# Slot scores transposed in one float32r product, and a running sum scanned along tokens, in a hybrid attention layer on one Trainium2 core

## The reference, cut to what matters

```python
s = hs @ Ws1.T @ Ws2.T + bs2                      # rank 16, then 16 heads x 64 slots
s = clip(s, -32, 32)                              # per head: [tokens, 64]
z = cumlogsumexp(s, axis=tokens); es = exp(s); enz = exp(-z)
A = tril(q @ k.T) * scale
ok = enz * (A @ es)
qv = softmax(ok)
W2 = tril((qv * enz) @ es.T)
o = W2 @ v                                        # then RMS norm, gate, @ Wo.T
```

## Time and profile before

| what | value |
|---|---|
| median of 3 runs | 822.07 us |
| the profiled execution's own time | 823.12 us |
| its span | 821.3 us |
| PE busy | 777.2 us, 95% |
| VectorE busy | 582.5 us, 71% |
| ScalarE busy | 435.3 us, 53% |
| GpSimd busy | 285.7 us, 35% |
| mean granted TensorE clock | 0.976 |
| chain that ended last | PE 90%, DVE 6%, POOL 1%, ACT 1% |

### The profile page before, as it was taken

The page is one execution under the profiler, slowest core; times in us unless marked ns, Lnnn a source line. Parts: engine busy times, 40 slices in busy tenths (PEclk is TensorE's granted clock), DMA queues, the critical chain, the costliest instruction groups (busy, mean ns, idle before and its releaser), DMA issues.

```text
span 821.3 us, 14494 instructions
## 1 busy us (share of the span) xinstructions
PE 777.2 (95%) x4571; PEld 660.5 (80%) x4571; DVE 582.5 (71%) x1502; ACT 435.3 (53%) x1188; POOL 285.7 (35%) x291
## 2 busy tenths in 40 slices
PE   7899999999999995799999999999999999999963
PEld 6788888888888884478888888888888888888852
DVE  4555545555555557869887988798888788887786
ACT  3455565555556542465656466556564665555420
POOL 6221010201101014435536346355364463563222
PEclk8999999999999998899999999999999999999997
DMA  7110101101010100100101001001001010000001
GB/s 229 36 52 6 46 13 38 49 2 51 13 38 13 51 1 14 53 1 13 53 0 38 25 13 51 0 13 51 0 20 44 13 51 0 13 0 0 1 1 52
DMA packets 23654, 23.76 MB, mean 29 GB/s; under 512 B 2369, under 2 KB 23361, under 8 KB 23506
## 3 DMA queue, kind: packets, MB, share of 16 engines
q1 hardware_dynamic: 23090, 22.98, 8.9%
q10 hardware_dynamic: 544, 0.52, 0.2%
HBM read 22.45 MB, written 1.05 MB: 29 GB/s over the span
## 4 chain that ended last, share of the span: by engine, by line
PE 90%; DVE 6%; POOL 1%; ACT 1%; issue 1%; DMA 0%; DVEq 0%; ACTq 0%; POOLq 0%
PE ps L1277 22%; PE ps L1493 11%; PE ps L1386 7%; PE ps L1284 5%; PE ps L1307 5%; PE ps L1505 3%; PE ps L1350 3%; PE ps L1391 3%; PE ps L1326 3%; PE ps L1530 3%; PE ps L1517 2%; PE ps L1547 2%; PE ps L1549 2%; PE ps L1548 2%; PE ps L1506 2%; PE ps L1519 2%
## 5 line engine op out<-in xcount | busy, mean ns | idle before, releaser
L1277 PE MATMUL ps<-xT_hi,w_hi 128*128 128x512 f32 x256 | 110.4, 431 | 3.9 <-DVE rot L1013 3.6
L1277 PE MATMUL ps<-xT_hi,w_lo 128*128 128x512 f32 x256 | 102.0, 398 | 0.0
L1277 PE MATMUL ps<-xT_lo,w_hi 128*128 128x512 f32 x256 | 101.5, 397 | 0.0
L1043 DVE TENSOR_TENSOR wt<-ps,const 128x384 f32<-128x384 f32 x128 | 68.3, 555 | 41.7 <-PE ps L1506 21.9
L383 POOL TENSOR_TENSOR w_lo<-w_raw,w_hi 128x512 fp32r<-128x512 f32 x32 | 40.8, 1286 | 155.7 <-ACT w_hi L536 155.7
L438 POOL TENSOR_TENSOR rot_s<-rot_s,const 128x512 f32<-128x512 f32 x64 | 82.0, 1293 | 21.2 <-ACT rot_s L679 21.2
L581 ACT ACTIVATE wt<-wt,negmax 128x128 f32<-128x128 f32 (+1 forms) x128 | 56.6, 443 | 28.1 <-DVE negmax L907 28.1
L895 DVE TENSOR_TENSOR v<-ps,bv_b 128x256 f32<-128x256 f32 x64 | 27.1, 423 | 51.8 <-PE ps L1284 51.8
L698 ACT ACTIVATE v<-ps 128x256 f32<-128x256 f32 x64 | 24.5, 382 | 72.6 <-PE ps L1493 72.3
L1032 DVE RECIPROCAL enz<-zs 128x128 f32<-128x128 f32 x64 | 60.4, 944 | 1.0 <-ACT zs L685 1.0
L1277 PEld LDWEIGHTS ps<-xT_hi,w_hi 128*128 128x128 f32 x256 | 49.2, 192 | 13.3 <-issue 4.5
(11 more groups left out here) (172 smaller groups left out, 2252.3 us busy)
## 6 DMA issues: line engine op xcount, KB each, us to landing
w_raw<-a_w_q SPq DMA_DIRECT2D x8, 256.0 KB, 2.6
wv<-a_w_v SPq DMA_DIRECT2D x8, 256.0 KB, 3.5
wo<-a_w_o SPq DMA_DIRECT2D x8, 256.0 KB, 2.7
w_raw<-b_Wq SPq DMA_DIRECT2D x8, 256.0 KB, 2.6
w_raw<-b_Wk SPq DMA_DIRECT2D x8, 256.0 KB, 3.3
wc<-b_Wv SPq DMA_DIRECT2D x8, 256.0 KB, 3.5
wc<-b_Wg SPq DMA_DIRECT2D x8, 256.0 KB, 3.7
wo<-b_Wo SPq DMA_DIRECT2D x8, 256.0 KB, 2.6
```

Source lines behind the costliest of these rows:

```text
L1043: d.tensor_tensor(dst, src[:, 0:384], tri3, ALU.mult).then_inc(done, 1)
L1277: ins = mm(PJ[n[0]], w[:, m, c, h * P:(h + 1) * P], x[:, c, cols], start=(t == 0), stop=(t == len(terms) - 1))
```

## The change

The rank-16 product is written three times into 96 PSUM rows. `s1s` holds in float32r the rounded values (rows 0 to 31 and 64 to 95, with a row of ones for the bias) and the remainders (rows 32 to 63); `ws2s` holds the rounded weights twice and their remainders once. One product with the pair's 128 columns of `ws2s` (copied by GpSimd to `ws2p`) gives the scores of 128 slots x 512 tokens, slots on partitions. Clip and exponential are then in that layout, so the exponential writes `esT` directly; `et` transposes it back to `es`. VectorE sums along tokens with two scans of 256; `z` is four transposes of the result. The tasks change their order, and with it their banks: on TensorE and ScalarE `et` takes the place that `z` had in the even step, `z` runs on TensorE between out_group and `k1`, ScalarE reads it out as the first thing of the odd step, and the odd step's `et` is gone. SyncE issues five small loads for `ws2` (which now shares memory with `enz`) in place of two, and GpSimd clears 96 rows of it and not `s1`. ScalarE writes all three groups of `s1s` (`s1_copy`, with the ones as its bias `s1_one`), and VectorE overwrites the middle group (`s1_tail`).

```diff
-B_TASKS = ["s", "q0", "q1", "z", "k0", "k1", "c0", "c1", "c2", "et", "c3"]
+B_TASKS = ["s", "q0", "q1", "et", "k0", "z", "k1", "c0", "c1", "c2", "c3"]
...
@@ GpSimd
+            g.tensor_tensor(s1_one[:, :], ident[:, RANK:RANK + 1], ident[:, 2 * S_GROUP + RANK:2 * S_GROUP + RANK + 1],
+                            ALU.add).then_inc(ws1x_done, 1)
+            for r in range(S_ROWS // S_GROUP):
+                g.tensor_copy(ws1x[:, :, r * S_GROUP:r * S_GROUP + RANK], ws1[:, :, :]).then_inc(ws1x_done, 1)
-            def exp_tail(phase, half):
-                pool.wait_ge(b_es_hi, phase + 1)
-                g.tensor_tensor(es_lo[:, :].rearrange("p (t m) -> p t m", t=HT), es[:, HT * half:HT * half + HT, :],
-                                es_hi[:, :].bitcast(F32).rearrange("p (t m) -> p t m", t=HT), ALU.subtract).then_inc(b_es_lo, 1)
+            def pair_slots(i):
+                g.tensor_copy(ws2p[0:S_ROWS, :], ws2s[0:S_ROWS, bass.ds(i * P, P)].bitcast(F32)).then_inc(b_ws2p, 1)
...
                         if b == 1 and not last:
                             split_tail(b_, i + 1, 1)
+                            pool.wait_ge(b_.proj_ps, slot_ps(i, 1, 0))
+                            pair_slots(i + 1)
@@ ScalarE
+            s.activation(ws2s[0:S_ROWS, :], ws2[0:S_ROWS, :], ACT.Copy).then_inc(ws2_hi, 1)
             with act.Fori(0, PAIRS - 1) as i:
                 a_body(i, False)
...
-                    s.activation(es[:, tl, :], clip.rearrange("p (t m) -> p t m", t=HT), ACT.Exp).then_inc(b_es, 1)
-                    act.wait_ge(b_es, phase + 1)
-                    s.activation(es_hi[:, :].rearrange("p (t m) -> p t m", t=HT), es[:, tl, :], ACT.Copy).then_inc(b_es_hi, 1)
+                    s.activation(esT[:, half * HALF:(half + 1) * HALF], clip, ACT.Exp).then_inc(b_est, 1)
...
-                    s.activation(esT[:, half * HALF:(half + 1) * HALF], PJ[bank], ACT.Copy).then_inc(b_.proj_evac[bank], 1)
+                    s.activation(es[:, tl, :], PJ[bank].rearrange("p (t m) -> p t m", t=HT), ACT.Copy).then_inc(b_.proj_evac[bank], 1)
@@ VectorE
+            def s1_tail(b):
+                rows, cols = slice(S_GROUP, 2 * S_GROUP), slice(b * T, (b + 1) * T)
+                dve.wait_ge(s1_hi, b + 1)
+                d.tensor_tensor(s1s[rows, cols], ps[rows, ffns[0].banks[b], 0:T], s1s[rows, cols].bitcast(F32),
+                                ALU.subtract).then_inc(s1_done, 1)
...
-            ffn_quant(0, 2)
+            ffn_range(0, 2)
+            s1_tail(0)
+            s1_tail(1)
+            ffn_round(0, 2)
...
+            def b_sums(phase, half):
+                dve.wait_ge(b_est, phase + 1)
+                for t in range(2):
+                    o = half * HALF + t * T
+                    d.tensor_tensor_scan(esumT[:, t * T:(t + 1) * T], esT[:, o:o + T], esT[:, o:o + T], 0.0, ALU.add, ALU.max
+                                         ).then_inc(b_esum, 1)
@@ VectorE, b_body, even step
-                        b_recip(None, b // 2, 3)
+                        b_recip(None, b // 2, 2)
...
                             b_rope_cos(n(2), 1, 0)
-                            b_recip(n(3), half, 0)
+                        b_recip(None, b // 2, 3)
...
                         if rest:
+                            b_sums(phase, half)
                             b_rope_cos(n(4), 0, 1)
@@ VectorE, b_body, odd step
-                            b_recip(None, half, 1)
+                            b_recip(n(5), half, 0)
...
-                            b_gate(n(8), phase, 2, half)
+                            b_gate(n(9), phase, 2, half)
+                            b_recip(None, half, 1)
                         if nxt:
                             b_okn_max(x + b + 1, (b + 1) % B, 2 * i + (b + 1) // 2)
...
-                        if rest:
-                            b_recip(None, half, 2)
@@ TensorE
                 if name == "s":
-                    for t in range(HT):
-                        tile = HT * half + t
-                        ins = mm(PJ[bank][:, t * P:(t + 1) * P], s1[:, tile * P:(tile + 1) * P],
-                                 ws2[:, bass.ds(pair * P, P)], start=True, stop=True)
+                    pe.wait_ge(b_ws2p, pair + 1)
+                    ins = mm(PJ[bank], ws2p[0:S_ROWS, :], s1s[0:S_ROWS, half * HALF:(half + 1) * HALF], start=True, stop=True)
...
                 elif name == "z":
-                    pe.wait_ge(b_es_lo, phase + 1)
-                    for part in (es_hi, es_lo):
-                        mm(PJ[bank], sums[:, 0:P], part[:, :], start=(part is es_hi), stop=False)
-                        ins = mm(by_tile(PJ[bank])[:, :, 1, :], sums[:, P:2 * P], by_tile(part[:, :])[:, :, 0, :],
-                                 start=False, stop=(part is es_lo))
+                    pe.wait_ge(b_esum, 2 * phase + 2)
+                    for t in range(HT):
+                        ins = tr(PJ[bank][:, t * P:(t + 1) * P], esumT[:, t * P:(t + 1) * P], ident)
...
-            def b_ok(x, b, phase):
-                pe.wait_ge(b_es, phase + 1)
+            def b_ok(x, b, i, h):
+                bank, count = slot_done(i, h, B_TASKS.index("et"))
+                pe.wait_ge(b_.proj_evac[bank], count)
                 pe.wait_ge(b_sc, 2 * x + 2)
```

More of the change, by code:

```diff
@@ L49 @@
 RANK = 16
-BIAS_ROW = 32
+S_ROWS = 96
+S_GROUP = 32
 SCALE = float(P) ** -0.5
@@ L135, in layer_kernel @@
         ws1 = sb("ws1", [P, C, RANK])
-        s1 = sb("s1", [P, B * T])
-        ws2 = sb("ws2", [P, HEADS * M])
+        ws1x = sb("ws1x", [P, C, S_ROWS])
+        s1_one = sb("s1_one", [P, 1])
+        s1s = sb("s1s", [P, B * T], F32R)
+        ws2s = sb("ws2s", [P, HEADS * M], F32R)
+        ws2p = sb("ws2p", [P, P], F32R)
         rot = sb("rot", [P, 2, HALF])
         rot_s = sb("rot_s", [P, 2, HALF])
-        es_hi = sb("es_hi", [P, HALF], F32R)
-        es_lo = sb("es_lo", [P, HALF], F32R)
-        sums = sb("sums", [P, 2 * P], F32R)
+        esumT = sb("esumT", [P, HALF])
         zs = sb("zs", [P, HALF])
@@ L146, in layer_kernel @@
         enz = sb("enz", [P, TILES, 2 * M])
+        ws2 = enz[:, :, :].rearrange("p t m -> p (t m)")
         gt = sb("gt", [P, 2, 2 * P])
@@ L321, in _ @@
             sp.dma_start(gw[:, :], b_gw.rearrange("(p o) -> p o", o=1)).then_inc(small_ld, 16)
-            sp.wait_ge(init_done, 3)
-            sp.dma_start(ws2[0:RANK, :], b_ws2).then_inc(small_ld, 16)
-            sp.dma_start(ws2[BIAS_ROW:BIAS_ROW + 1, :], b_bs2.rearrange("(o n) -> o n", o=1)).then_inc(small_ld, 16)
+            sp.wait_ge(init_done, 2)
+            for g in range(S_ROWS // S_GROUP):
+                sp.dma_start(ws2[g * S_GROUP:g * S_GROUP + RANK, :], b_ws2).then_inc(ws2_ld, 16)
+            for g in (0, 2):
+                row = g * S_GROUP + RANK
+                sp.dma_start(ws2[row:row + 1, :], b_bs2.rearrange("(o n) -> o n", o=1)).then_inc(ws2_ld, 16)
             sp.dma_start(const[:, K_TRI:K_END], consts[:, K_TRI:K_END]).then_inc(table_ld, 16)
@@ L992, in _ @@
                     tail(0, 3, 5)
+            low = slice(2 * S_GROUP, S_ROWS)
+            dve.wait_ge(ws2_hi, 1)
+            d.tensor_tensor(ws2s[low, :], ws2[low, :], ws2s[low, :].bitcast(F32), ALU.subtract).then_inc(ws2_done, 1)
             with dve.Fori(0, PAIRS - 1) as i:
@@ L1141, in b_body @@
                         if rest:
[L1142 to L1143 removed]
+                            b_gate(n(7), phase, 0, half)
+                            b_recip(n(5), half, 0)
                         if nxt:
@@ L1146, in b_body @@
                         if rest:
-                            b_gate(n(7), phase, 1, half)
+                            b_gate(n(8), phase, 1, half)
                         if last and b == 3:
@@ L1190, in _ @@
             ln_stats(2, 3, ffns[0].acc, 4)
-            b_rope_cos(n0(5), 1, 1)
-            b_recip(None, 0, 1)
+            b_recip(n0(5), 0, 0)
+            b_rope_cos(n0(6), 1, 1)
             b_rope_add(4, 1, 1, 0)
             ln_scale(2, 3)
-            b_gate(n0(6), 0, 0, 0)
+            b_gate(n0(7), 0, 0, 0)
+            b_recip(None, 0, 1)
             tail(1, 2, ffns[0].banks[2])
-            b_gate(n0(7), 0, 1, 0)
+            b_gate(n0(8), 0, 1, 0)
             b_scores(0)
             tail(1, 3, ffns[0].banks[3])
-            b_gate(n0(8), 0, 2, 0)
+            b_gate(n0(9), 0, 2, 0)
             b_okn_max(0, 0, 0)
             b_slots(0)
-            b_recip(None, 0, 2)
+            s1_tail(2)
+            s1_tail(3)
             with dve.Fori(0, PAIRS - 1) as i:
@@ L1524, in b_w2_product @@
                 pe.wait_ge(b_z, x + b + 1)
-                bank, count = slot_done(i, b // 2, B_TASKS.index("et"))
-                pe.wait_ge(b_.proj_evac[bank], count)
+                pe.wait_ge(b_est, 2 * i + b // 2 + 1)
                 t0 = b * T
@@ L1600, in b_body @@
                         if rest:
+                            b_task(i, 1 + b // 2, B_TASKS.index("z"), half, phase)
```

(1 more changed line is left out.)

66 lines of the change are left out of this document (33 added, 33 removed).

## The result

| | us | of before, with 95% interval |
|---|---|---|
| the kernel before, 4 runs | 821.52 (817.59 to 822.13) | |
| the changed kernel, 4 runs | 877.65 (874.91 to 878.66) | 1.0689 [1.0647, 1.0731] |
| the profiled execution of it | 877.59, span 875.7 | |

What follows compares the result with a forecast made beforehand. TensorE's gapless list was taken to bound the loop. 14 halves at 1.86 + 0.6 us, plus smaller terms for GpSimd's copy, loop start and last pair, made 38.7 us: 860.8 us forecast, range 846 to 884.

Steps and rivals of the forecast that it cites:

- The scores `s`: Even step: the shorter `s` takes some 0.8 us off TensorE's list, but W2 waits for zT instead; counted as nothing.
- GpSimd's copy: Even step: GpSimd's new copy for the next pair, some 0.5 us long, costs 0.1 us a pair.
- `et` in the place of `z`: Even step: ok waits about 1 us for ScalarE's copy of `es`, starting at 590.95 in place of 590.50.
- `z` behind the scans: Between out_group and `k1`: TensorE's `z` waits for VectorE's two scans, so `k1` starts 1.86 us later.
- The odd step: `et` gone, -0.36 us, but out_tail behind the second reciprocal delays out_group's last two products: +0.6 us against before.
- Around the loop: Where b begins: ffn_round waits behind s1_tail, and scans and small tails enter; +2.0 us, between 0.5 and 3.5.
- the first half's +1.0: Last pair: its first half loses less than those inside the loop, since its output product is longer; +1.0 us.
- the tail's 0.5: From the last pair's first half to the end: one more reciprocal +0.9, odd step without out_tail -0.4.
- at one beat an element: Rival: the scan runs at plain-operation rate, 0.54 us less in each of 15 halves; 852.7 us, chance 0.13.
- at the reciprocal's rate: Rival: each scan takes 1.9 us, 2.5 us more in 15 halves; 898 us, chance 0.05.
- The clock: Rival: waits in each half drop TensorE's clock to 1.2 GHz, 22 us more; 883 us, chance 0.14.
- Faster: Rival: sums ready in time, ok's wait covered, so TensorE's list is 1.3 us less in 16 halves; 803 us, chance 0.09.

Runs made afterwards that it cites:

- e4: The kernel before with only one of the four products of each `s`: 821.73 us, 1.0017 of before.
- e9: The kernel before with two of the four products of `z`: 819.99 us, 0.9997 of before.
- e12: The changed kernel with GpSimd's rope and qp products cut to 8 columns of each: 865.28 us, 1.0552 of before.
- e1: The changed kernel with the two scans of each half issued ahead of the score masks on VectorE: 847.36 us, 1.0319 of before.
- e10: The kernel before with one of four products of `s`, two of four of `z`, one of four transposes of `et`: 819.78 us, 0.9996 of before.
- e2: The changed kernel with the odd step's reciprocals moved, none left before the operations on ok: 865.75 us, 1.0532 of before.
- e3: The changed kernel with GpSimd's copy of the first pair's columns ahead of its wait for the feed-forward: 871.93 us, 1.0632 of before.
- e5: The changed kernel with the edits of e1, e2 and e3 together: 831.28 us, 1.0118 of before.
- e6: e5 with zT copied between the read-outs of v and gate, and GpSimd's later copies ahead of a split: 828.73 us, 1.0088 of before.
- e7: e6 with `k0` ahead of ok in the even step, and the first half's scans behind ffn_out: 823.90 us, 1.0030 of before.

## Why the prediction was right, and where its sizes were off

**The scores `s`: right.** It was counted at nothing, for zT's sake, and in the changed kernel W2 starts 1.35 us after `qp` (614.07 to 615.42), where it started after 1.36. e4 shows it alone. GpSimd's copy, put at 0.1 us a pair, costs nothing: the wait for it (0.48) lies in the same gap, and the half with it (30.71) is no longer than the one without (30.79). Its length was taken at 0.5 us and is 0.29.

**`et` in the place of `z`: the right sum for a wrong reason.** I had ok wait for the copy of `es`. It doesn't: the ok product of the even step reads the `es` of the half already in use, copied long before. ok waits for the masks of the scores (1548, 0.21 us), which begin when the scores are done and end 1.2 us later, whatever TensorE does between (e9). The gap is 0.45 us in place of the predicted 1 us, and none of it counted, since it lies inside the wait for `z`.

**`z` behind the scans: the right mechanism, short by a fifth.** The scans start 6.00 us after the masks (590.58 to 596.58); rows 5 gave 6.02. A scan that runs alone takes 0.67 us (e12), and 0.68 was the price taken, by two operations one after the other. The second of each half takes up to 1.15, and that was missed:

```profile
L1055 DVE TENSOR_TENSOR_SCAN esumT<-esT x6: 683/914/1147, 596.6 to 658.7; 128x256 f32<-128x256 f32 x6
```

(min, median and max ns of six). It runs beside GpSimd's qp product, and the rope product behind it takes 1.67 us where 1.29 is usual. From the scores to `k1` it is 9.08 us (589.72 to 598.80) where it was 6.72 (588.38 to 595.10), 2.36 more in place of the predicted 1.86; 0.45 of the difference is the scan, 0.05 the transposes of `z` (0.41 in place of 0.36). The whole even step grew as much, 16.90 us on the mean against 14.52. In e1, which moves the scans to a time when GpSimd has nothing to do, 2.0 of this are gone, and the transposes' 0.4 stay.

**The odd step: right.** +0.6 was predicted, and it is +0.75 (13.82 against 13.07 on the mean): out_tail stands behind the reciprocal (609.75, 612.07) and holds the last products for 0.64 us, where I had put a wait of 1 us. The -0.36 for `et` was wrong, as e10 shows (0.19 at most) and e2 (0.17), without effect here, since out_tail ends last.

**Around the loop: the step that failed.** The +2.0 us where b begins are +10.0. I followed VectorE and ScalarE there and not GpSimd's order: its first copy stands behind a wait for the feed-forward's rounding and a split of 2.34 us. e3 takes 4.1 of the 8 us away, and e5 and e6, which have the same edit, as much. The rest has to do in part with the first half's scans, for which `z` waits 3.88 us: e12, which frees VectorE's operations from GpSimd's, brings 3.7 us there. e7, with these scans earlier, has 1.4 less than e6, but that is no more than the stretch differs by between executions (35.0 to 36.7 us in the kernel before and the experiments on it). How these parts add up is open, and 4.7 us are left in e7. In the last pair, the first half's +1.0 is +1.1. Of the tail's 0.5, put at 0.9 for the reciprocal less 0.4, its step b = 2 shows +0.5 (15.85 us between the `qp` transposes, 15.88 in e3, 15.34 before); the other 1.8 of the measured 2.3 aren't there in e3 (27.0 us from the last `qp` to the end, 27.2 before, 29.0 in the changed kernel). Nor can the 2.7 us by which b begins earlier be laid to the change. That the total of the profiled span fits the medians owes something to these two, which nearly cancel.

**The rivals.** The scan isn't at one beat an element (852.7; by the terms given for it 0.51 us a half and 853.2) nor at the reciprocal's rate (898). The clock stayed at 1.00 in every window of the loop, so 883 is out, though the time came near it: by contention in the scans and at the start of b. *Faster* at 803 wanted the sums and the reciprocals in time and ok's wait covered. e5 meets the first two, e7 all three, and what comes out is 831 and 824. So its price was wrong as well: 1.3 us of list less a half isn't worth 1.3 us. The Trainium skill (DVE: opcode table, instruction layouts, handler registers and perf-mode slots, section 6, Datapath and trigger behaviour) has the scan at half throughput. The trace agrees: 0.67 us for 256 elements is the time of a plain operation of 512 (0.68), where one of 256 takes 0.43.

## What to carry to other kernels

In a kernel whose busiest engine shows no gaps, its work can still be standing in the place of waits: before pricing a cut, list for the instruction behind it what else it needs and when that ends; here three cuts of 1.5 us a half in all were worth 0.1. Price a move by the place of the moved work in every engine's order, GpSimd's included: here a 0.29 us copy behind a wait it didn't need cost some 4 us, and two scans late in VectorE's order cost 2 us a half. Where a new VectorE operation has two inputs in SBUF, look at what GpSimd does at that time. And before a difference outside the repeated part of a kernel is laid to a change, compare profiles of other kernels with the same program there: here such stretches differed by 2 to 5 us with an unchanged program.

## What the runs showed of the hardware

A scan slows down beside GpSimd, and GpSimd beside it. In the changed kernel the two scans take 1.75 us from 596.58 on while GpSimd's qp product (597.05, 0.74 us) and rope product (597.75, 1.67 in place of 1.29) run; in e1 and e12, 1.26. The numbers fit turns, not a shared rate: by its own length the first scan is done at about 597.2, the second ends at 598.33, 0.54 us after the qp product (597.79), and the rope product ends at 599.4, 1.1 us after the second scan. No run parted the qp product from the rope product.

The same is seen where b begins, on plain operations with two inputs in SBUF, in the changed kernel and already in the kernel before:

```profile
345.85 1.29 POOL L453 TENSOR_TENSOR rot_s<-rot_s,const 128x512 f32<-128x512 f32 x1 [0.94 <-ACT rot_s L692]
346.10 1.59 DVE L1042 TENSOR_TENSOR qT<-rot,rot_s 128x512 f32<-128x512 f32 x1
```

```profile
335.17 2.39 POOL L383 TENSOR_TENSOR wc_lo<-wc,wc_hi 128x1024 fp32r<-128x1024 f32 x1 [6.39 <-DVE qb L859]
336.51 1.60 DVE L874 TENSOR_TENSOR y<-y,fb_b 128x512 f16<-128x512 f32 x1
```

VectorE's operation, 0.69 us by itself, ends 0.55 us after GpSimd's in both (347.69 and 347.14; 338.11 and 337.56), however long it had to stand. In e12, with the rope product cut short, the first of them takes 0.69. And the one that starts first is the one that isn't held: in e3 the same pair starts the other way round, VectorE keeps its 0.69, and GpSimd takes 1.76 in place of 1.29 (VectorE's next operation of this kind, at 341.20, then ends 0.54 us after GpSimd's):

```profile
340.60 0.69 DVE L1044 TENSOR_TENSOR qT<-rot,rot_s 128x512 f32<-128x512 f32 x1
```

```profile
340.68 1.76 POOL L460 TENSOR_TENSOR rot_s<-rot_s,const 128x512 f32<-128x512 f32 x1 [1.27 <-ACT rot_s L694]
```

The Trainium skill (SBUF — State Buffer, section "Who interferes with whom") says that a VectorE instruction with two SBUF inputs contends with a GpSimd instruction that reads SBUF, and (section "SBUF: two separate sides") that the one that starts first has the port pair for its whole length while the other blocks. The traces agree for these pairs, with up to 0.9 us for VectorE (1.59 in place of 0.69) and 0.4 to 0.5 for GpSimd. They don't for GpSimd's operations on 128x2 elements: one that starts at 319.03 and takes 0.72 us in the changed kernel leaves VectorE's, which starts at 319.45, its usual 0.69. The masks and og's products (1073, 1097), which read one input in PSUM, run beside two rope products from 591.00 on, and those take 2.50 us together, their usual length.
